# Norm factors as one VectorE operation and an inverse square root on GpSimd, and P in operations of 512 columns, in a one-core decoder layer

## Chip, cores and metric

The kernel runs on one core of a Trainium2 chip. The metric is the device time of one execution in microseconds. The kernel before took 3062.6 us (median of three runs, 3057.56 to 3067.12).

## The reference

One decoder layer on x of 4 x 512 tokens and 512 features: a gated delta-rule attention, a WKV recurrence over a second input and a routed feed-forward layer, each followed by a residual sum and a layer norm. The change touches only the attention:

```
q, k = l2norm(q) * DK**-0.5, l2norm(k)          # l2norm(x) = x / sqrt(sum(x*x) + 1e-6)
for each token:                                 # 32 heads, state Sm of 128 x 128 each
    Sm = Sm * exp(g)
    delta = (v - k @ Sm) * beta
    Sm = Sm + outer(k, delta)
    o = q @ Sm
og = o * silu(z)
on = og * rsqrt(mean(og*og) + EPS) * norm_w     # over the 128 features of a head
out = on @ w_out
```

The kernel works with q and k as they come and puts their lengths in later. With n2 = sum(q*q) + 1e-6 and ss = sum(og*og) of the unscaled output, the factor on og is

    1 / sqrt(ss / 128 + EPS * 128 * n2)  =  sqrt(128) / sqrt(ss + EPS * 128**2 * n2)

## The kernel before

Setup splits x into a high and a low part for exact products in three matmuls and makes the gates' decays. Then attention runs in 64 rounds and one tail does WKV, feed-forward and the three norms.

An attention unit s is one of 16 key heads (with its two value heads) and one of four chunks of 128 tokens, for all four batches. Round r of the loop works on three units at once: the state, the output and the output projection of unit r ("state"), the block inverse of unit r+1 ("solve"), and the projections, the convolution and the gates of unit r+2 ("ahead"). Each engine has its own in-order list of steps for a round, written out by hand (for TensorE from line 597, ScalarE 829, VectorE 1111, GpSimd 1213); the engines meet in semaphores that count upwards. The loop's order on each queue is all the scheduling there is.

The steps around the change:

- *gram* (VectorE, line 909): n2 is the lengths of the four k and four q per token (columns 4 to 7 are q's), r2 its reciprocal, cf and cfl the factors of delta. Then M (line 933), eight operations, and P (line 941), four operations: the products q k of PSUM times the decays E. M goes to DRAM and comes back as N in blocks; *base* (line 944) waits for it. TensorE's *by_token* (line 422) waits for each half of P, as it writes into the banks that P reads.
- *output* and *update* (lines 1029, 1047): O, the gated output, and the next state. ScalarE's *lengths* (line 746) squares O into ss.
- *taps* (line 1080): the convolution, three operations of 128x512 for each of the four projections j. Those of j = 1 stand partly ahead of the factors: all three in rounds with r mod 4 of 0 or 3, otherwise one ("early", line 1128).
- *factors* (VectorE, line 1060): f from ss and r2 in four dependent operations on 128x8. GpSimd's *factors* (line 1179) raises f to 0.5 and writes ron. ScalarE's *normed* (line 756, operation in line 763) scales O by ron into R. TensorE's *turn* (line 547, operation in line 551) transposes R, ScalarE's and VectorE's *turn* take it out of PSUM with a factor normw, and *out* (line 554) multiplies by w_out.
- behind the factors on VectorE: the remaining taps of j = 1 and those of j = 2, then *turn_T* (line 985) and *x_part* (line 994) of the block inverse. Xc (line 998) is what TensorE's *y_part* (line 449, operation in line 457) waits for; X itself comes from *x_part* on TensorE (lines 439 and 446).
- ScalarE has the SiLU of j = 1 (*silu*, line 799, operation in line 810) right ahead of *normed*; it waits for the last tap of j = 1.
- Line 409 transposes k and q of the next unit; its second half waits for Ut (line 702), the end of the block inverse. GpSimd also splits weights (line 1204) and keeps the convolution's halo (1193, 1199).

Of the kernel before, what the change touches and what calls it, by code (L numbers as in the profile page):

```python
# [9 lines left out]
ALU = mybir.AluOpType  # L10
# [3 lines left out]
B, S, D = 4, 512, 512  # L14
HV, HK, DH = 32, 16, 128
HJ = HV // HK
C = 128
# [11 lines left out]
EPS_NORM, EPS_LN = 1e-6, 1e-5  # L29
# [20 lines left out]
def decoder_kernel(nc, a, out):  # L50
    with ExitStack() as ctx:
        t, names = {}, []

        def sb(scope, name, *shape, dtype=F32):
            full = f"{name}_{len(names)}"
            names.append(full)
            t[name] = scope.enter_context(nc.sbuf_tensor(full, list(shape), dtype))
            return t[name]
# [9 lines left out]
        sb(ctx, "acc", 128, B, NC, D)  # L68
        sb(ctx, "eye4", 128, 4, 128)
        sb(ctx, "half", 128, 8)  # L70
        sb(ctx, "mhalf", 128, 4)
        sb(ctx, "ln", 128, 3, B, 12)
        for name, rows_, size in (("wkv_w", 128, KT), ("wkv_u", 128, KT), ("w_rows", KT, 128)):
            sb(ctx, name, rows_, size)
# [57 lines left out]
def setup(nc, a, t, banks, scratch, on):  # L132
# [95 lines left out]
    def vector(dve):  # L228
        def low(c):
            dve.wait_ge(on["xs_hi"], c + 1)  # L230
            dve.tensor_tensor(split("lo", c), t["xT"][:, c], split("hi", c), ALU.subtract).then_inc(on["xs_lo"], 1)

        for c in range(NC):
            low(c)
        dve.wait_ge(on["exs"], 1)
        dve.tensor_scalar(negA[:], negA[:], -1.0, None, ALU.mult).then_inc(on["gates"], 1)
        dve.wait_ge(on["exs"], 4)
        dve.tensor_scalar(wr[:], ex[:], 1.0, None, ALU.add).then_inc(on["w_plus"], 1)
        dve.wait_ge(on["ln"], 1)
        dve.tensor_scalar(wr[:], wr[:], -1.0, None, ALU.add).then_inc(on["gates"], 1)  # L240
        dve.wait_ge(on["gates"], 2)
        dve.tensor_scalar(tiny[:], wr[:], 0.0, None, ALU.is_equal).then_inc(on["gates"], 1)
        dve.wait_ge(on["gates"], 3)
        dve.tensor_tensor(wr[:], wr[:], tiny[:], ALU.add).then_inc(on["gates"], 1)
        dve.wait_ge(on["gates"], 4)
        dve.tensor_tensor(lg[:], lg[:], tiny[:], ALU.add).then_inc(on["gates"], 1)
        dve.wait_ge(on["gates"], 5)
        dve.reciprocal(wr[:], wr[:]).then_inc(on["gates"], 1)
        dve.wait_ge(on["gates"], 6)
        dve.tensor_tensor(lg[:], lg[:], wr[:], ALU.mult).then_inc(on["gates"], 1)  # L250
        dve.wait_ge(on["gates"], 7)
        dve.tensor_tensor(lg[:], lg[:], ex[:], ALU.mult).then_inc(on["gates"], 1)
        dve.wait_ge(on["gates"], 8)
        dve.scalar_tensor_tensor(out=yrow[:], in0=yrow[:], scalar=0.0, in1=lg[:], op0=ALU.max, op1=ALU.add).then_inc(on["gates"], 1)
        dve.memset(wr[:], 0.0).then_inc(on["gates"], 1)
        dve.wait_ge(on["gates"], 10)
        dve.wait_ge(on["exs"], 5)
        dve.tensor_copy(chunks(wr)[:, :, 0:1], chunks(ex)[:, :, 0:1]).then_inc(on["gates"], 1)
        dve.wait_ge(on["gates"], 11)
        dve.memset(chunks(ex)[:, :, 0:1], 0.0).then_inc(on["gates"], 1)  # L260
        dve.wait_ge(on["gates"], 12)
        dve.tensor_tensor_scan(cum[:], ex[:], wr[:], 0.0, ALU.mult, ALU.add).then_inc(on["cums"], 1)
        dve.wait_ge(on["cums"], 1)
        dve.tensor_copy(t["ends"][:], chunks(cum)[:, :, C - 1])

    with nc.Block() as block:  # L266
        block.sync(sync)
# [6 lines left out]
def attention(nc, a, t, banks, scratch, on):  # L274
# [7 lines left out]
    by2 = lambda ap: ap.rearrange("p (b j) -> p b j", j=HJ)  # L282
# [20 lines left out]
    n2, r2, nk = (lambda s: of(s, 0)), (lambda s: of(s, 8)), (lambda s: of(s, 16, 4))  # L303
    cf, cfl = (lambda s: of(s, 24)), (lambda s: of(s, 32))
    ncum = lambda s, b, j: tok[:, b, s % NC, 0, s // NC, j:j + 1]
    two = lambda name, s: t[f"{name}{s % 2}"]
# [350 lines left out]
    def scalar(act):  # L657
# [88 lines left out]
        def lengths(s):  # L746
            act.wait_ge(on["SD"], 2 * grown(s + 1))
            if s:
                act.wait_ge(on["f"], 4 * (s - 1) + 1)
            for half in range(2):  # L750
                act.wait_ge(on["og"], 2 * s + half + 1)
                for u in range(4 * half, 4 * half + 4):
                    op = act.activation(De[:, u // HJ, u % HJ], O[:, u // HJ, u % HJ], ACT.Square, accum_out=t["ss"][:, u:u + 1])
                op.then_inc(on["ss"], 1)
# [74 lines left out]
        for r in range(-3, NS):  # L829
# [27 lines left out]
            if state:  # L857
                lengths(r)
# [30 lines left out]
    def vector(dve):  # L889
# [19 lines left out]
        def gram(s):  # L909
# [13 lines left out]
            for half in range(2):  # L923
                b4 = solve_bank(half)[:].rearrange("p (b k s) -> p b k s", b=2, k=2)
# [5 lines left out]
                for i in range(2):  # L930
                    b = 2 * half + i
                    for j in range(HJ):
                        op = dve.scalar_tensor_tensor(out=t["M"][:, b, j], in0=b4[:, i, 0], scalar=cf(s)[:, 2 * b + j:2 * b + j + 1],
                                                      in1=t["E"][:, j, b], op0=ALU.mult, op1=ALU.mult)
                op.then_inc(on["M"], 1)
            for half in range(2):
                b4 = solve_bank(half)[:].rearrange("p (b k s) -> p b k s", b=2, k=2)
                if half == 0 and s >= 2:
                    dve.wait_ge(on["PD"], 2 * (s - 2) + 2)
                for j in range(HJ):  # L940
                    op = dve.tensor_tensor(two("P", s)[:, 2 * half:2 * half + 2, j], b4[:, :, 1], t["E"][:, j, 2 * half:2 * half + 2], ALU.mult)
                op.then_inc(on["P"], 1)

        def base(s):

# [112 lines left out]
                op.then_inc(on["S_next"], 1)  # L1058

        def factors(s):  # L1060
            f, r2q = t["f"], r2(s)[:, 4:8].unsqueeze(2).broadcast_to([128, B, HJ])
            dve.wait_ge(on["ss"], 2 * s + 2)
            dve.wait_ge(on["r2"], s + 1)
            if s:
                dve.wait_ge(on["ron"], s)
            dve.tensor_tensor(by2(f[:]), by2(t["ss"][:]), r2q, ALU.mult).then_inc(on["f"], 1)
            dve.wait_ge(on["f"], 4 * s + 1)
            dve.tensor_scalar(f[:], f[:], 1.0 / DH, EPS_NORM * DH, ALU.mult, ALU.add).then_inc(on["f"], 1)
            dve.wait_ge(on["f"], 4 * s + 2)
            dve.reciprocal(f[:], f[:]).then_inc(on["f"], 1)  # L1070
            dve.wait_ge(on["f"], 4 * s + 3)
            dve.tensor_tensor(by2(f[:]), by2(f[:]), r2q, ALU.mult).then_inc(on["f"], 1)

        def out(s, b):
            if s + b == 0:
# [35 lines left out]
        for r in range(-2, NS):  # L1111
# [3 lines left out]
            if solve:  # L1115
                gram(r + 1)
# [49 lines left out]
    def gpsimd(pool):  # L1166
# [10 lines left out]
            pool.tensor_tensor(t["wout_lo"][:, j], wout_raw[:, j], t["wout_hi"][:, j], ALU.subtract).then_inc(on["wout_lo"], 1)  # L1177

        def factors(s):
            pool.wait_ge(on["f"], 4 * s + 4)  # L1180
            if s:
                pool.wait_ge(on["on"], 2 * s)
            pool.tensor_tensor(t["ron"][:], t["f"][:], t["half"][:], ALU.pow).then_inc(on["ron"], 1)  # L1183

        def before(s, j):
            xb, halo, n = t["xb"][:, j], t["halo"][:, j], 4 * s + j
# [19 lines left out]
        def norm1(c):  # L1206
            st = t["ln"][:, c]
            pool.wait_ge(on["ln_stats"], 10 * c + 10)
            pool.tensor_tensor(st[:, :, 9], st[:, :, 8], t["mhalf"][:], ALU.pow).then_inc(on["ln_rstd"], 1)
            pool.wait_ge(on["ln_rstd"], 2 * c + 1)  # L1210
            pool.tensor_tensor(st[:, :, 11], st[:, :, 9], st[:, :, 10], ALU.mult).then_inc(on["ln_rstd"], 1)

# [584 lines left out]
```

## Time and profile before

| | |
|---|---|
| median of three runs | 3062.6 us |
| the profiled execution | 3062.48 us |
| its span | 3060.7 us |
| setup | 0 to about 54 us |
| attention loop | about 54 to 2699 us |
| tail | about 2699 us to the end |

The span is what the profiler sees between the first and the last instruction. An engine's idle time stands in front of the instruction that follows it, with the instruction that ended it. Operations of one engine can overlap by some tens of nanoseconds, so that merged rows ("x4") take less than the count times the mean.

### The profile page before, as it was taken

Reading aid. Unit: us, or ns where it says so; the run is one execution under the profiler, and the core shown is the slowest. Engines: PE = TensorE matmul, PEld = TensorE weight load, DVE = VectorE, ACT = ScalarE, POOL = GpSimd, SP = SyncE. Lnnn points to the kernel's source line nnn. Section 1 sums busy time; section 2 is a strip of 40 time slices with the busy share of each in tenths; the row PEclk is TensorE's granted clock in tenths of the full one; section 3 lists DMA queues with packets and bytes.
Section 4 is the critical chain, followed back from the end, with each engine's and each line's share of the span. In section 5 each row is a group of like instructions: output and inputs, shape, how many; then the busy total and the mean of one; then the engine's idle time right before and its main releaser. Section 6 shows DMA issues by size and latency. Waiting matters only on the chain. (4 is left out here: it accounts for less than half of the span.)

```text
span 3060.7 us, 78831 instructions
## 1 busy us (share of the span) xinstructions
PE 2884.2 (94%) x28584; PEld 2369.2 (77%) x28584; DVE 2663.7 (87%) x6377; ACT 1941.1 (63%) x6331; POOL 613.6 (20%) x902
## 2 busy tenths in 40 slices
PE   6899999999999999999999999999999999749998
PEld 4788887888888888888888888888888888636665
DVE  4698988999898889888989898988889898879995
ACT  3576666676767676666766666666676766544442
POOL 1121212121212112121212111212121221132221
PEclk9899999999999999999999999999999999869999
DMA  6434433343334343434334333334344433120000
GB/s 255 136 97 110 122 105 117 103 122 108 106 100 124 106 123 101 122 95 118 90 108 123 109 116 108 115 109 121 86 120 110 123 102 101 32 93 25 28 19 18
DMA packets 498474, 315.75 MB, mean 103 GB/s; under 512 B 314150, under 2 KB 453542, under 8 KB 480424
## 3 DMA queue, kind: packets, MB, share of 16 engines
q1 hardware_dynamic: 498088, 310.70, 34.6%
q8 instruction: 231, 3.78, 0.5%
q14 instruction: 155, 1.27, 0.1%
HBM read 243.07 MB, written 50.73 MB: 96 GB/s over the span
## 5 line engine op out<-in xcount | busy, mean ns | idle before, releaser
L1088 DVE SCALAR_TENSOR_TENSOR conv<-xb,convw,conv 128x512 f32<-128x512 f32 x768 | 592.0, 774 | 81.0 <-ACT conv L797 66.2
L580 PE MATMUL bank<-x_hi,w_hi 128*128 128x512 f32 x1024 | 429.7, 420 | 9.7 <-PEq L266 6.3
L580 PE MATMUL bank<-x_hi,w_lo 128*128 128x512 f32 x1024 | 403.2, 394 | 0.0
L580 PE MATMUL bank<-x_lo,w_hi 128*128 128x512 f32 x1024 | 400.5, 391 | 0.0
L791 ACT ACTIVATE xb<-bank 128x512 f32<-128x512 f32 x256 | 161.3, 630 | 302.7 <-PE bank L580 278.1
L592 PE MATMUL bank<-w_hi,x_hi 128*128 128x256 f32 x1024 | 304.4, 297 | 3.8 <-ACT conv L797 3.7
L592 PE MATMUL bank<-w_hi,x_lo 128*128 128x256 f32 x1024 | 290.4, 284 | 1.0 <-issue 1.0
L592 PE MATMUL bank<-w_lo,x_hi 128*128 128x256 f32 x1024 | 290.5, 284 | 0.0
L1171 POOL TENSOR_TENSOR small<-small,half 128x4 f32<-128x4 f32 x64 | 64.5, 1007 | 1034.2 <-DVE small L915 1034.2
L1199 POOL COPY halo<-xb 128x12 f32<-128x12 f32 x256 | 90.2, 352 | 839.3 <-ACT xb L791 839.0
L580 PEld LDWEIGHTS bank<-x_hi,w_hi 128*128 128x128 f32 x1024 | 194.1, 190 | 47.1 <-issue 9.0
L565 PE MATMUL bank<-wout_hi,onT_hi 128*128 128x512 f32 x512 | 230.0, 449 | 0.4 <-issue 0.4
L580 PEld LDWEIGHTS bank<-x_hi,w_lo 128*128 128x128 f32 x1024 | 193.3, 189 | 43.6
L580 PEld LDWEIGHTS bank<-x_lo,w_hi 128*128 128x128 f32 x1024 | 194.5, 190 | 37.5
L592 PEld LDWEIGHTS bank<-w_hi,x_hi 128*128 128x128 f32 x1024 | 195.8, 191 | 13.9 <-ACT conv L797 6.2
L565 PE MATMUL bank<-wout_hi,onT_lo 128*128 128x512 f32 x512 | 202.9, 396 | 0.0
L565 PE MATMUL bank<-wout_lo,onT_hi 128*128 128x512 f32 x512 | 202.7, 396 | 0.0
L592 PEld LDWEIGHTS bank<-w_lo,x_hi 128*128 128x128 f32 x1024 | 196.5, 192 | 2.5
L592 PEld LDWEIGHTS bank<-w_hi,x_lo 128*128 128x128 f32 x1024 | 196.5, 192 | 1.2 <-issue 1.2
L810 ACT ACTIVATE conv<-conv 128x512 f32<-128x512 f32 x128 | 80.1, 626 | 171.0 <-DVE conv L1088 169.0
L797 ACT ACTIVATE conv<-bank,convw 128x512 f32<-128x512 f32 x256 | 183.7, 718 | 3.2 <-DMA convw<-in_conv_w 3.2
L763 ACT ACTIVATE R<-O,ron 128x128 f32<-128x128 f32 x512 | 156.7, 388 | 32.9 <-POOL ron L1183 30.3
(276 smaller groups left out, 7643.6 us busy)
## 6 DMA issues: line engine op xcount, KB each, us to landing
x_hi<-x_hi_scratch SPq DMA_DIRECT2D x63, 1024.0 KB, 5.0
x_lo<-x_lo_scratch SPq DMA_DIRECT2D x63, 1024.0 KB, 8.2
E<-decay_scratch SPq DMA_DIRECT2D x64, 512.0 KB, 5.2
M_scratch<-M SPq DMA_DIRECT2D x128, 256.0 KB, 2.4
w_raw<-in_w_proj SPq DMA_DIRECT2D x64, 384.0 KB, 8.5
U<-Ut SPq DMA_DIRECT2D x256, 64.0 KB, 2.0
w_raw<-in_w_out SPq DMA_DIRECT2D x32, 256.0 KB, 3.0
Mt<-M_scratch SPq DMA_DIRECT2D x256, 32.0 KB, 1.9
```

The lines of the kernel that those rows point to most:

```text
L565: mm = pe.matmul(banks[4 + b][:], lhsT=t[f"onT_{p}"][:, j, b, :], rhs=t[f"wout_{q}"][:, j, :], start=i + j == 0, stop=i + j == len(PAIRS))
L580: mm = pe.matmul(banks[j % 2][:].rearrange("p (b t) -> p b t", b=B), lhsT=t[f"w_{p}"][:, k, j, :], rhs=t[f"x_{q}"][:, k], start=i == 0, st ...
L592: mm = pe.matmul(banks[half][:, i * 256:(i + 1) * 256], lhsT=t[f"x_{p}"][:, k, b, :], rhs=t[f"w_{q}"][:, k, 4:6, :], start=n == 0, stop=n ...
L763: op = act.activation(R[:, b, j], O[:, b, j], ACT.Copy, scale=t["ron"][:, HJ * b + j:HJ * b + j + 1])
L791: act.activation(xb[:, :, TAPS - 1:], bank[:].rearrange("p (b t) -> p b t", b=B), ACT.Copy).then_inc(on["xb"], 1)
L797: act.activation(y, bank[:], ACT.Copy, scale=t["convw"][:, j, TAPS - 1:]).then_inc(on["y"], 1)
L810: act.activation(dst, y3, ACT.Silu).then_inc(on["silu"], 1)
L1088: dve.scalar_tensor_tensor(out=y3, in0=xb[:, :, i:i + C], scalar=t["convw"][:, j, i:i + 1], in1=y3, op0=ALU.mult, op1=ALU.add).then_inc(on ...
L1171: pool.tensor_tensor(nk(s), n2(s)[:, 0:4], t["half"][:, 0:4], ALU.pow).then_inc(on["nk"], 1)
L1199: pool.tensor_copy(halo, xb[:, :, C:C + TAPS - 1]).then_inc(on["save"], 1)
```

## The change

The four operations of *factors* on VectorE become one scalar_tensor_tensor, f = n2 * (EPS * 128 * 128) + ss. GpSimd raises it to -0.5 in place of 0.5, on the same shape. The missing factor sqrt(128) goes into normw, which setup scales once. The operand mhalf grows to eight columns. The semaphore f now counts one per round in place of four, and its waits follow. The step waits for n2 in place of r2; both are written in *gram* long before. And P is made in two operations of 128x512 in place of four of 128x256; the first operand is read from PSUM with the two value heads j as a broadcast dimension.

```diff
@@ setup, vector
+        dve.wait_ge(on["d_in"], 32)
+        dve.tensor_scalar(t["normw"][:], t["normw"][:], float(np.sqrt(DH)), None, ALU.mult)
@@ attention, scalar, lengths
-                act.wait_ge(on["f"], 4 * (s - 1) + 1)
+                act.wait_ge(on["f"], s)
@@ attention, vector, gram
-                for j in range(HJ):
-                    op = dve.tensor_tensor(two("P", s)[:, 2 * half:2 * half + 2, j], b4[:, :, 1], t["E"][:, j, 2 * half:2 * half + 2], ALU.mult)
-                op.then_inc(on["P"], 1)
+                dve.tensor_tensor(two("P", s)[:, 2 * half:2 * half + 2], b4[:, :, 1].unsqueeze(2).broadcast_to([128, 2, HJ, C]),
+                                  t["E"][:, :, 2 * half:2 * half + 2].rearrange("p j b s -> p b j s"), ALU.mult).then_inc(on["P"], 1)
@@ attention, vector, factors
-            f, r2q = t["f"], r2(s)[:, 4:8].unsqueeze(2).broadcast_to([128, B, HJ])
             dve.wait_ge(on["ss"], 2 * s + 2)
-            dve.wait_ge(on["r2"], s + 1)
+            dve.wait_ge(on["n2"], s + 1)
             if s:
                 dve.wait_ge(on["ron"], s)
-            dve.tensor_tensor(by2(f[:]), by2(t["ss"][:]), r2q, ALU.mult).then_inc(on["f"], 1)
-            dve.wait_ge(on["f"], 4 * s + 1)
-            dve.tensor_scalar(f[:], f[:], 1.0 / DH, EPS_NORM * DH, ALU.mult, ALU.add).then_inc(on["f"], 1)
-            dve.wait_ge(on["f"], 4 * s + 2)
-            dve.reciprocal(f[:], f[:]).then_inc(on["f"], 1)
-            dve.wait_ge(on["f"], 4 * s + 3)
-            dve.tensor_tensor(by2(f[:]), by2(f[:]), r2q, ALU.mult).then_inc(on["f"], 1)
+            dve.scalar_tensor_tensor(out=by2(t["f"][:]), in0=n2(s)[:, 4:8].unsqueeze(2).broadcast_to([128, B, HJ]), scalar=EPS_NORM * DH * DH,
+                                     in1=by2(t["ss"][:]), op0=ALU.mult, op1=ALU.add).then_inc(on["f"], 1)
@@ attention, gpsimd, factors
-            pool.wait_ge(on["f"], 4 * s + 4)
+            pool.wait_ge(on["f"], s + 1)
-            pool.tensor_tensor(t["ron"][:], t["f"][:], t["half"][:], ALU.pow).then_inc(on["ron"], 1)
+            pool.tensor_tensor(t["ron"][:], t["f"][:], t["mhalf"][:], ALU.pow).then_inc(on["ron"], 1)
```

## Rows read from the trace of the kernel before

**Rows 1.** The page: each engine's busy us, share of the span and instructions.
```profile
PE 2884.2 (94%) x28584; PEld 2369.2 (77%) x28584; DVE 2663.7 (87%) x6377; ACT 1941.1 (63%) x6331; POOL 613.6 (20%) x902
```

**Rows 2.** Busy us of PE, PEld, DVE, ACT, POOL; granted clock; DMA share, GB/s.
```profile
130.00:2640.00 2510.00, 2438.77 (x26414) 2067.77 (x26414) 2251.62 (x5617) 1716.90 (x5848) 494.38 (x739) 1.00 0.38 109
```

**Rows 3.** TensorE's waits from 130 to 2640 us: total us, times, longest.
```profile
PE bank L457 <- DVE Xc L998: 20.7, 30, 1.2
PE bank L551 <- ACT R L763: 19.5, 26, 1.4
PE bank L409 <- ACT Ut L702: 10.0, 15, 0.7
PE bank L427 <- DVE P L941: 5.0, 16, 1.0
```

**Rows 4.** Timeline of one round: start us, us, instruction, idle before it and releaser.
```profile
1197.13 0.16 DVE L1066 TENSOR_TENSOR f<-ss,small 128x8 f32<-128x8 f32 x1
...
1197.85 3.77 DVE L1088 SCALAR_TENSOR_TENSOR conv<-xb,convw,conv 128x512 f32<-128x512 f32 x5
1198.02 2.08 POOL L1183 TENSOR_TENSOR ron<-f,half 128x8 f32<-128x8 f32 x1 [1.49 <-DVE f L1072]
...
1199.42 0.63 ACT L810 ACTIVATE kq<-conv 128x512 f32<-128x512 f32 x1 [1.03 <-DVE conv L1088]
1200.13 2.45 ACT L763 ACTIVATE R<-O,ron 128x128 f32<-128x128 f32 x8
...
1201.55 0.63 PE L551 MATMUL bank<-eye,R 128*128 128x128 f32 x4 [0.78 <-ACT R L763]
1201.90 0.39 DVE L998 TENSOR_TENSOR Xc<-bank,level 128x256 f32<-128x256 f32 x1
...
1202.34 0.76 PE L457 MATMUL bank<-Xc,Uc 32*32 32x32 f32 x64 [0.16 <-DVE Xc L998]
```

**Rows 5.** Timeline: first and last of 46 idle rounds; one round with ScalarE idle.
```profile
186.42 0.75 PE L457 MATMUL bank<-Xc,Uc 32*32 32x32 f32 x64 [1.21 <-DVE Xc L998]
...
265.76 2.45 ACT L763 ACTIVATE R<-O,ron 128x128 f32<-128x128 f32 x8 [1.62 <-POOL ron L1183]
...
267.18 0.63 PE L551 MATMUL bank<-eye,R 128*128 128x128 f32 x4 [0.87 <-ACT R L763]
...
2577.47 0.26 PE L457 MATMUL bank<-Xc,Uc 32*32 32x32 f32 x6 [1.18 <-issue]
```

**Rows 6.** Powers on GpSimd, by line (min/median/max ns) and group (mean ns).
```profile
L1183 POOL TENSOR_TENSOR ron<-f,half x64: 1635/2076/2081, 140.3 to 2685.2; 128x8 f32<-128x8 f32 x64
L1209 POOL TENSOR_TENSOR ln<-ln,mhalf x3: 1008/1010/1010, 2640.3 to 2684.0; 128x4 f32<-128x4 f32 x3
L1171 POOL TENSOR_TENSOR small<-small,half 128x4 f32<-128x4 f32 x64 | 64.5, 1007 | 1034.2 <-DVE small L915 1034.2
L1725 POOL TENSOR_TENSOR a<-base_e,a 128x4 f32<-128x4 f32 x1 | 1.4, 1379 | 0.7 <-DVE a L1524 0.7
```

**Rows 7.** VectorE's groups by shape, the whole span or the loop: busy us, mean ns.
```profile
L1078 DVE TENSOR_TENSOR acc<-bank,acc 128x512 f32<-128x512 f32 x256 | 169.0, 682 | 7.3 <-PE bank L565 5.4
L941 DVE TENSOR_TENSOR P<-bank,E 128x256 f32<-128x256 f32 x256 | 90.2, 416 | 0.0
L979 DVE TENSOR_TENSOR prods<-T,W 64x512 f32<-64x512 f32 x64 | 77.5, 1211 | 2.2
L954 DVE SCALAR_TENSOR_TENSOR prods<-N,T 64x8 f32<-64x8 f32 x61 | 9.6, 158 | 0.0
```

**Rows 8.** Timeline: P, and two operations of the 512-column form in a row.
```profile
1253.92 1.26 DVE L1078 TENSOR_TENSOR acc<-bank,acc 128x512 f32<-128x512 f32 x2
...
1258.93 1.41 DVE L941 TENSOR_TENSOR P<-bank,E 128x256 f32<-128x256 f32 x4
```

**Rows 9.** VectorE's waits over the whole span: total us, times, longest.
```profile
DVE T L951 <- DMA N<-M_scratch: 57.5, 58, 3.2
```

**Rows 10.** Busy time and granted clock of one stretch, columns as in rows 2.
```profile
349.40:352.80 3.40, 3.40 (x45) 2.81 (x44) 2.10 (x5) 1.52 (x3) 0.00 (x0) 0.50 0.43 96
```

More of the change, by code:

```diff
@@ L70, in decoder_kernel @@
         sb(ctx, "half", 128, 8)
-        sb(ctx, "mhalf", 128, 4)
+        sb(ctx, "mhalf", 128, 8)
         sb(ctx, "ln", 128, 3, B, 12)
@@ L1208, in norm1 @@
             pool.wait_ge(on["ln_stats"], 10 * c + 10)
-            pool.tensor_tensor(st[:, :, 9], st[:, :, 8], t["mhalf"][:], ALU.pow).then_inc(on["ln_rstd"], 1)
+            pool.tensor_tensor(st[:, :, 9], st[:, :, 8], t["mhalf"][:, 0:B], ALU.pow).then_inc(on["ln_rstd"], 1)
             pool.wait_ge(on["ln_rstd"], 2 * c + 1)
```

## The prediction

> **What bounds the kernel now.** I read the totals of the page first, then the busy time by stage, then TensorE's waits, then single rounds of the timeline. TensorE is busy 94% of the span and VectorE 87% [rows 1]. The middle of the attention loop, from 130 to 2640 us, is 2510 us long, and TensorE is busy for 2438.8 us of it at a granted clock that rounds to full speed [rows 2]. So in 62 rounds of about 40 us only 71 us are not TensorE's own work. Work that this change removes from VectorE is not worth its own length: it is worth what it takes out of these 71 us, and nothing else. The reader should therefore ask of each edit which of TensorE's waits it shortens.
>
> The table of waits names them [rows 3]. The longest two are the product of the block inverse (line 457) waiting for VectorE's Xc, 20.7 us in 30 waits, and the transposes of the normed output (line 551) waiting for ScalarE's R, 19.5 us in 26 waits. Then come 10.0 us for Ut (line 409) and 5.0 us for P (line 427).
>
> One round shows that the first two hang on one place in VectorE's order of work [rows 4]. VectorE starts the norm factors at 1197.13 and begins the next tap at 1197.85, so the four dependent operations take 0.72 us. GpSimd starts its power at 1198.02 and ScalarE the scaling of R at 1200.13, right behind it; TensorE, idle for 0.78 us, starts its transposes at 1201.55. VectorE itself runs through five taps, the transpose and Xc without a gap, and Xc (1201.90) releases line 457 at 1202.34 after a further 0.16 us of idle. In another kind of round there is no idle ahead of Xc either, but ScalarE has nothing else to wait for: it stood 1.62 us until the factors of GpSimd were there [rows 5].
>
> **The change, part by part.** *Norm factors.* Before, the operations start at 1197.13 and the next VectorE operation at 1197.85. Afterwards there is one small operation. The nearest row is the scalar_tensor_tensor of line 954, 158 ns [rows 7]; a broadcast operand does not show in it, but line 1066 has one and its row in the round is 0.16 us too [rows 4]. As line 1066 does with an operation that does not depend on it, the next tap can begin a little before the end, at about 0.09 us. So VectorE's queue moves 0.72 - 0.09 = 0.63 us earlier from there on, and so does the start of the power: both ends of the chain, R and Xc, move by the same 0.63 us. The price from both sides: if the next tap has to wait for the full end and a semaphore, the shift is 0.55; it can't be above 0.72.
>
> *The power.* It has the same shape, 128x8, but the exponent is -0.5 and the operand another. Its time is 2076 ns in nearly all rounds and 1635 ns at the least [rows 6]. The pattern of the round explains both: taps follow each other at 3.77/5 = 0.754 us, the power starts 0.17 after the first, so 1.64 us of its own would end at 1199.66, and it ends at 1200.10, where the third tap ends (1197.85 + 3 x 0.754 = 1200.11) [rows 4]. It ends with a tap because it waits for one. As tap and power move together by 0.63, this phase stays, and so does 2.08. The exponent: a power by -0.5 of 128x4 took 1008 to 1010 ns three times, in line with 1007 for the power by 0.5 of that shape; a power of the same 128x4 with other operands took 1379 [rows 6]. I take no change, and keep 37% as the upper bound for a rival.
>
> Here the Trainium skill has a rule (page "SBUF — State Buffer", section "SBUF: two separate sides"): a GpSimd operation and a VectorE operation with two SBUF inputs hold a shared port pair exclusively, and the loser is blocked for the whole instruction. The trace agrees that GpSimd loses up to 0.44 us, but not that a power blocks taps: the five taps beside it keep 0.754 us each. Under the strict rule the power would push one tap back by its full 1.64 us, before and after alike.
>
> *What the 0.63 us are worth.* The waits have to be taken one by one, since a wait of 0.16 us can give back only 0.16. I listed every idle of TensorE in front of lines 551 and 457 from 130 to 2640 us: 46 rounds have one, the first at 186.42, the last at 2577.47 (one of two whose releaser the view leaves open; I count both) [rows 5]. In each round the gain is the smaller of 0.63 and the idle at both lines together. Of the 26 rounds with an idle at line 551, 18 reach 0.63, which is 11.3 us, and eight give 0.22 to 0.61, together 3.5 us. Of the 20 with one at line 457 alone, 11 (about 1.2 us each) give 0.63, 6.9 us, and nine give 0.16, 1.5 us. Sum: 23.2 us. In the other rounds VectorE only gets ahead and waits later: it already stands 57.5 us in 58 rounds for the block N from DRAM [rows 9], a wait that hangs on M and not on anything that is made shorter here.
>
> What is late next? ScalarE's SiLU of the second projection ends at 1200.05, only 0.05 before the power does [rows 4]. It was itself released by a tap that stands behind the factors, so it moves too. GpSimd could be the next limit only if it were not idle before the power; it waits for f before it. For line 409 I count nothing: its chain starts behind line 457 and moves rigidly with it.
>
> *P.* Four operations of 256 columns, 416 ns each, become two of 512 with one operand in PSUM; line 1078 has that form and takes 682 ns, the same form at 128x512 [rows 7]. Durations would say 1664 - 1364 = 0.30 us per round. But operations that don't depend on each other overlap: four of P take 1.41 us on the engine and two of line 1078 take 1.26 [rows 8]. So it is 0.15 us. It moves the block solve nowhere, since VectorE waits for N right after [rows 9]. It shortens line 427's waits, 16 of them, 5.0 us in all [rows 3]: 16 x 0.15 = 2.4 us, between 0 and 5.0.
>
> The Trainium skill's VectorE page ("VectorE: DVE Perf Modes", section "The TRN2 errata — SBUF-src ops pay a fixed extra latency per instruction") gives 120 cycles of fixed cost for an operation that reads PSUM, at 0.96 GHz. An estimate from that page: two operations fewer save 0.25 us a round, 16 us in 64 rounds if VectorE were the bound. The rows of this case show 0.15 us of engine time, and most of that in front of a wait.
>
> *The rest.* The extra scaling of normw in setup is one column wide, behind the last scan; I count 0. The operand mhalf of eight columns costs nothing.
>
> *The clock.* TensorE's granted clock falls to half (1.2 of 2.4 GHz) for 3.4 us just behind rounds with long idle: from 349.40 to 352.80 it is 0.50 [rows 10], and there are five such stretches between 130 and 2640 us. Each follows within 3 us a round where TensorE stood 1.5 to 2.2 us in front of these two lines (the first of them 0.91 and then 1.21 us); two other rounds with 2.0 and 2.4 us have none. A stretch costs at most 3.4/2 = 1.7 us, five 8.5 us. The change takes 0.63 off the idle ahead of each. From 0 to 8.5, I take half, 4.2 us.
>
> **Sum.** 23.2 + 2.4 + 4.2 = 29.8 us. The profiled execution took 3062.48 us (its span 3060.7), the median of the runs is 3062.6, so no correction between them: 3062.5 - 29.8 = 3032.7, say **3033 us**.
>
> **Rivals.**
> 1. *The gain comes, but the clock gives nothing or P nothing:* 3062.5 - 23.2 = 3039; with all five stretches gone and all of line 427's waits, 3062.5 - 36.7 = 3026. These are inside my forecast.
> 2. *ScalarE's order takes the wait over.* If its SiLU did not move, of line 551's rounds only those where ScalarE stood idle for the factors would gain, 15 of the 26 and 7.4 us; line 457 does not hang on ScalarE and keeps its 8.4: 3062.5 - 7.4 - 8.4 - 2.4 = 3044 us. For it: the two end 0.05 apart [rows 4]. Against it: the SiLU waits for a tap behind the factors. Chance 0.10.
> 3. *VectorE's gain is not in TensorE's waits:* they are filled by something that I don't see (a DMA, or the next wait in the round, such as line 409's), and only P's 2.4 us are left: 3060 us. For it: 71 us of idle in 2510 is little, and many chains run side by side. Against it: behind line 457 all that TensorE waits for starts from line 457 itself. Chance 0.12.
> 4. *Slower: the power on GpSimd.* If the new operands made it longer, the end of a tap sets how much. Up to 0.44 us more is free, since it ends at the same tap; by the 37% of the row of 1379 ns it would grow by 0.6 and end one tap later, so that R comes 0.75 - 0.63 = 0.12 us later than now: 26 x 0.12 = 3 us lost against 8.4 + 2.4 gained, 3054 us. From 1.2 us more on it ends two taps later, R comes 0.87 us late, and at least the 26 rounds lose that: 3062.5 + 22.6 - 2.4 = 3083 us, the gain at line 457 being hidden behind 551. Against it: the 1009 ns at -0.5. Chance 0.04, of which 0.03 slower.
> 5. *P costs more than its columns.* 512-element operations with awkward access take 1211 ns here (line 979) against 682 [rows 7]. P would then take about 2.3 instead of 1.41 us, and in the 16 rounds with no cover 0.9 us each are lost: 14 us, 3062.5 - 23.2 + 14 = 3053 us. Its inner runs are 128 contiguous columns in both forms, which speaks against it. Chance 0.04.
>
> **How the numbers follow.** Forecast 0.70, rival 2 0.10, rival 3 0.12, rival 4 0.04, rival 5 0.04. The predicted time is the forecast's. The range has to hold 8 in 10: from 3023 (all terms at their upper bound, 3026, less some scatter of the runs, which spread over 9.6 us) to 3055 (rivals 2 and 5 inside, which leaves out rivals 3 and 4 and some of the forecast's own error). Below 0.3%, 9.2 us, this measurement can't tell from no change: 3053.4 to 3071.8 is the same. Faster holds the forecast but for 0.03 given away, rival 2 and half of rival 5: 0.79. The same holds rival 3, half of 5, the small case of 4 and the 0.03: 0.18. Slower is the large case of 4: 0.03.
>
> **What the profile after would show.** One row of about 0.16 us in the place of lines 1066 to 1072, and the next tap about 0.1 us after its start. The power at 2.08 us as before and its exponent without effect. The waits of line 551 fall from 19.5 to about 6 us and those of line 457 from 23 (with the two open ones) to about 14, since in rounds with both the one at 457 stays while its moment moves; line 427's from 5.0 to about 3. P in two rows of about 0.68 us. TensorE's busy time from 130 us to the end of the loop unchanged but for fewer stretches of 0.5 clock, while the stretch itself gets shorter; VectorE's wait for N longer by some 0.15 us a round. I am wrong if the waits at 551 and 457 stay although the factors are 0.63 us earlier, if the power's duration moves, or if the waits go and others (409, 439) grow by as much.

## The result, and the profile after

The changed kernel takes 3034.8 us (median of four executions, 3031.6 to 3037.9), the kernel before 3061.3 us beside it: ratio 0.9923, 95% interval 0.9906 to 0.9940. (The ratios are those on record; they are not the quotients of the two medians, which would be 0.9913 here.) Measured again in another session it was 3031.7 us beside 3063.1, and 0.9900 (0.9881 to 0.9919). The prediction was 3033 us, in a range from 3023 to 3055. The profiled execution took 3034.04 us, with a span of 3032.3 us against 3060.7. All ratios leave out one single execution, the sixth of experiment 6, which took 15768 us for a reason that nothing here shows.

The page's busy times and the stretch of the loop that answers to [rows 1, 2]:

```profile
PE 2877.5 (95%) x28584; PEld 2367.5 (78%) x28584; DVE 2624.8 (87%) x6058; ACT 1937.2 (64%) x6331; POOL 617.3 (20%) x902
130.00:2612.00 2482.00, 2433.13 (x26424) 2067.13 (x26423) 2214.55 (x5310) 1714.38 (x5853) 498.14 (x739) 1.00 0.38 110
```

VectorE lost 39 us of work, and the span 28 us. TensorE did the same 28584 matmuls. In the loop it stood idle for 49 us where it had stood for 71.

TensorE's waits from 130 to 2620 us, for [rows 3] (line 459 was 457, 553 was 551, 411 was 409, 429 was 427):

```profile
PE bank L459 <- DVE Xc L999: 13.4, 19, 1.2
PE bank L411 <- ACT Ut L704: 10.4, 15, 0.7
PE bank L553 <- ACT R L765: 4.5, 14, 0.7
PE bank L459 <- issue: 3.6, 3, 1.7
PE bank L429 <- DVE P L942: 3.6, 16, 0.6
```

The two waits that were forecast to fall fell: for R from 19.5 to 4.5 us, for Xc from 20.7 to 13.4. The wait for Ut, which was said to move rigidly with line 457, did not change (10.0 and 10.4 us).

The timeline of one round, for [rows 4]:

```profile
1187.02 0.19 DVE L1066 SCALAR_TENSOR_TENSOR f<-small,ss 128x8 f32<-128x8 f32 x1
1187.13 3.78 DVE L1083 SCALAR_TENSOR_TENSOR conv<-xb,convw,conv 128x512 f32<-128x512 f32 x5
1187.29 2.09 POOL L1178 TENSOR_TENSOR ron<-f,mhalf 128x8 f32<-128x8 f32 x1
...
1189.54 2.44 ACT L765 ACTIVATE R<-O,ron 128x128 f32<-128x128 f32 x8
...
1191.36 0.60 PE L553 MATMUL bank<-eye,R 128*128 128x128 f32 x4
...
1191.89 0.75 PE L459 MATMUL bank<-Xc,Uc 32*32 32x32 f32 x64
```

From the start of f to the first tap there are 0.11 us (0.72 before), and the power takes 2.09 us (2.08 before). Both of the idles in front of lines 551 and 457 are gone. R starts 2.52 us after f, where it was 3.00: it gained 0.48 us and not 0.61.

The power is not the same in every round. In 17 of the 64 (12 in the second profile of this kernel) it starts 0.8 us or more after f and takes 1.63 us. In 15 of them (all of the kind called 0 below) GpSimd's own copy of the halo comes in between, which before had been done by the time f was ready. The copy in one such round before, and the same place after:

```profile
300.29 0.19 POOL L1199 COPY halo<-xb 128x12 f32<-128x12 f32 x1 [1.55 <-ACT xb L791]
```

```profile
300.71 0.16 DVE L1066 SCALAR_TENSOR_TENSOR f<-small,ss 128x8 f32<-128x8 f32 x1
300.79 2.32 DVE L1083 SCALAR_TENSOR_TENSOR conv<-xb,convw,conv 128x512 f32<-128x512 f32 x3
300.85 0.74 POOL L1194 COPY halo<-xb 128x12 f32<-128x12 f32 x1 [1.58 <-ACT xb L793]
301.55 1.64 POOL L1178 TENSOR_TENSOR ron<-f,mhalf 128x8 f32<-128x8 f32 x1
```

The copy, 0.19 us long before, now starts 0.06 us into a tap and ends 0.05 us behind it, after 0.74 us, and the power starts behind it. Its end comes 2.47 us after f's start in place of 2.36, so this costs some 0.1 us of R's shift in these rounds.

And P, for [rows 8]:

```profile
1247.67 1.28 DVE L942 TENSOR_TENSOR P<-bank,E 128x512 f32<-128x512 f32 x2
...
1248.40 1.26 PE L429 MATMUL bank<-eye,conv 128*128 128x128 f32 x8 [0.20 <-DVE P L942]
```

The sharpest view is the length of a round, taken between two starts of line 439 (441 after) on TensorE. The same round of both kernels, first before, then after:

```profile
1482.24 0.25 PE L439 MATMUL bank<-Tc,M 32*32 32x32 f32 x6
1524.82 0.26 PE L439 MATMUL bank<-Tc,M 32*32 32x32 f32 x8
```

```profile
1466.78 0.45 PE L441 MATMUL bank<-Tc,M 32*32 32x32 f32 x32
1508.73 0.45 PE L441 MATMUL bank<-Tc,M 32*32 32x32 f32 x32
```

42.58 became 41.95: 0.63 us, the shift that was forecast for VectorE's queue. Rounds repeat in four kinds, numbered here from the first such start. The table has the median round of each kind, and the sum from the first start to the last but one, each from one profiled execution (kernels of the experiments stand here too, with the number of the experiment):

| kernel | kind 0 | kind 1 | kind 2 | kind 3 | 62 rounds |
|---|---|---|---|---|---|
| before | 38.51 | 40.19 | 42.58 | 39.61 | 2511.5 |
| after | 38.05 | 40.19 | 41.95 | 38.93 | 2482.2 |
| after, second time (3) | 38.18 | 40.19 | 41.96 | 39.06 | 2481.8 |
| factors alone (1) | 38.05 | 40.19 | 41.93 | 38.79 | 2472.3 |
| factors alone, second time (4) | 38.03 | 40.20 | 41.95 | 38.77 | 2482.6 |
| delay behind f (5) | 37.95 | 40.19 | 42.45 | 39.18 | 2493.5 |
| delay ahead of f (6) | 38.39 | 40.19 | 42.48 | 39.11 | 2502.5 |
| Xc one tap earlier (9) | 37.96 | 40.18 | 41.16 | 38.98 | 2465.3 |
| P twice (12) | 38.97 | 40.19 | 41.94 | 38.75 | 2484.4 |

Kind 1 has no wait at either line in 14 of its 16 rounds and gains nothing (40.19 both times): VectorE got ahead there and waited, its listed idle in the 16 rounds growing from 55.5 to 63.2 us. The other three kinds gain 8.4, 10.8 and 12.0 us; kind 1 loses 1.9, nearly all in two odd rounds. The sum is 29.3 us. (The first such start comes 1.9 us later than before, and what follows the last but one takes 1.1 us less; that makes the 28 us of the span.) The medians repeat to within 0.15 us from one execution of a kernel to the next, the sums do not: 2472.3 and 2482.6 us are the same kernel.

### The profile page after: what moved, and what is told of

It is laid out like the page before. It is cut to its first block and busy times, and to the rows that moved or that the text cites. A ratio compares the mean times of both kernels' runs of the same rounds, so it can differ in the third digit from the quotient of the medians.

```text
span 3032.3 us, 78512 instructions
## 1 busy us (share of the span) xinstructions
PE 2877.5 (95%) x28584; PEld 2367.5 (78%) x28584; DVE 2624.8 (87%) x6058; ACT 1937.2 (64%) x6331; POOL 617.3 (20%) x902
## 5 line engine op out<-in xcount | busy, mean ns | idle before, releaser
L1083 DVE SCALAR_TENSOR_TENSOR conv<-xb,convw,conv 128x512 f32<-128x512 f32 x768 | 591.9, 774 | 89.7 <-ACT conv L799 74.9
L1194 POOL COPY halo<-xb 128x12 f32<-128x12 f32 x256 | 103.7, 405 | 840.3 <-ACT xb L793 840.3
L1073 DVE TENSOR_TENSOR acc<-bank,acc 128x512 f32<-128x512 f32 x256 | 169.0, 681 | 7.5 <-PE bank L567 5.5
```

Source lines behind the costliest of these rows:

```text
L1073: dve.tensor_tensor(t["acc"][:, b, s % NC, :], banks[4 + b][:], t["acc"][:, b, s % NC, :], ALU.add).then_inc(on["acc"], 1)
L1083: dve.scalar_tensor_tensor(out=y3, in0=xb[:, :, i:i + C], scalar=t["convw"][:, j, i:i + 1], in1=y3, op0=ALU.mult, op1=ALU.add).then_inc(on ...
L1194: pool.tensor_copy(halo, xb[:, :, C:C + TAPS - 1]).then_inc(on["save"], 1)
```

## The experiments

**1. The factors alone** (P as before):

```diff
-                dve.tensor_tensor(two("P", s)[:, 2 * half:2 * half + 2], ...  # 512 columns
+                for j in range(HJ):
+                    op = dve.tensor_tensor(two("P", s)[:, 2 * half:2 * half + 2, j], b4[:, :, 1], t["E"][:, j, 2 * half:2 * half + 2], ALU.mult)
+                op.then_inc(on["P"], 1)
```

> The changed kernel with P as before, in four operations of 256 columns. Theory (the place of the factors in VectorE's order is what pays): about 25 us of the 26.5 stay, ratio to the kernel before 0.992 to 0.993 (3036 us), TensorE's waits for R and Xc as in the changed kernel (about 4.5 and 13 us), the wait for P back at 0.27 us each. Rival (the gain is VectorE's total load, of which P's operations are a part: P's rows fell from 90 to 82 us, the factors from 45 to 11): about four fifths of the gain, 3040 us, and the waits for R and Xc in between.

3029.9 us, ratio 0.9905 (0.9888 to 0.9922): the whole gain, without P's new form. TensorE's waits, 130 to 2610 us:

```profile
PE bank L459 <- DVE Xc L1000: 12.6, 18, 1.2
...
PE bank L429 <- DVE P L943: 4.7, 16, 0.6
...
PE bank L553 <- ACT R L765: 3.6, 12, 0.6
```

**2. P alone** (before.py with the two operations of 512 columns):

> The kernel before with only P in two operations of 512 columns. Theory: 1 to 2.4 us (3059 to 3060 us), the waits for P 0.20 instead of 0.27 us each, the waits for R and Xc as before (19.5 and 20.7 us) since VectorE waits for the block N behind P. Rival (VectorE's load counts): 5 us, the waits for R and Xc shorter.

3061.8 us, ratio 1.000 (0.9989 to 1.001). The waits for R and Xc are nearly those of before, and the wait for P fell all the same, from 5.0 us in 16 waits (130 to 2640 us):

```profile
PE bank L457 <- DVE Xc L997: 20.6, 30, 1.2
PE bank L551 <- ACT R L763: 17.1, 24, 1.4
...
PE bank L427 <- DVE P L940: 3.9, 16, 0.8
```

So P's part is worth nothing that can be measured; up to 3 us either way stay possible. Where its 0.14 us a round go is seen in VectorE's waits. Right behind P stand the taps of j = 0, and in 46 rounds (kinds 1 to 3) they wait for ScalarE's conv; the wait for N stands behind them. First before, then P alone, both from 130 to 2640 us:

```profile
DVE conv L1088 <- ACT conv L797: 44.5, 46, 1.0
```

```profile
DVE T L950 <- DMA N<-M_scratch: 54.2, 62, 3.5
DVE conv L1087 <- ACT conv L797: 51.1, 46, 1.1
```

The wait for conv is 45.2 and 45.1 us in the two executions with the factors alone and 50.9 and 50.8 in the two of the changed kernel, so it hangs on P's form. The wait for N (54.7 us before in this stretch) did not grow with P.

The first two measurements seemed to say that the 512 columns even cost something, 3029.9 us without them against 3034.8 with them, but they come from different sessions. So both were measured again, side by side on one chip.

**3. The changed kernel again, 4. the factors alone again:**

> The changed kernel unchanged, beside the one with the factors alone on the same chip. Theory: both within 3 us of each other, near 3035 and 3032 us; the number of stretches at half clock in the loop differs from kernel to kernel and takes or gives 1.7 us each. Rival (P in 512 columns costs something): the changed kernel is slower by 4 us or more with an interval clear of the other.

> The kernel with the factors alone again. Theory: 3030 to 3035 us, within 3 us of the changed kernel. Rival: 4 us or more faster than it, as the first measurement suggested (0.9905 against 0.9923).

3031.7 us (0.9900, 0.9881 to 0.9919) and 3036.2 us (0.9918, 0.9897 to 0.9939). Now the order is the other way round. The difference of 4 to 5 us between the two was scatter and not P.

**5. A delay behind the factors.** The changed kernel with three dependent operations of 0.2 us on a small tile of their own (three tensor_scalar on dum, 128x8, each waiting for the one before). The delay is work added.

```diff
             if state:
                 factors(r)
+                idle_ops(r)
```

> The changed kernel with three dependent small operations on a tile of their own (about 0.6 us) on VectorE right behind the factors. VectorE's load is that of before in time, R can come early only where ScalarE's SiLU does not wait for a tap behind them, Xc comes as late as before. Theory: only rounds with a wait for R and none for Xc gain, 7.2 us, and P's 1 to 2: 3052 us; the 1.2 us waits for Xc are back. Rival (the load counts, or everything hangs on Xc): 3059 us, as in the kernel with the delay ahead of the factors.

**6. The same delay ahead of the factors.**

> The same three operations ahead of the factors. Theory: R and Xc are as late as before, nearly all of the gain is gone: 3058 to 3060 us, the waits for R 19 us and for Xc 20 us. Rival (the gain came from fewer semaphore steps between VectorE and GpSimd or from the other operand of the power): it stays below 3050 us.

3045.5 us (0.9945, 0.9927 to 0.9964) with the delay behind f, 3051.1 us (median of five; 0.9960, 0.9946 to 0.9974) with the delay ahead of it. The executions of the two overlap (3037.1 to 3050.0 and 3044.6 to 3054.3), so that their times alone do not tell them apart for certain; both lie well above the factors alone in the same session (3029.9). Waits of the first, then of the second kernel, both 130 to 2610 us:

```profile
PE bank L459 <- DVE Xc L999: 22.2, 30, 1.4
...
PE bank L553 <- ACT R L765: 7.9, 10, 1.0
```

```profile
PE bank L459 <- DVE Xc L999: 20.6, 30, 1.2
PE bank L553 <- ACT R L765: 17.5, 26, 1.2
```

The waits are what the place says. With the delay ahead of the factors both are nearly back at their values of before, although f itself is still one operation and the power has its new operand. With the delay behind, Xc is as late as before and R is early. So neither the fewer semaphore steps nor VectorE's load made the gain, but the two moments at which f and Xc are there. The kinds of rounds show it for each of the two. Kind 0 waits for R and not for Xc: it is as short as in the changed kernel with the delay behind f (37.95 against 38.05), and nearly as long as before with the delay ahead of it (38.39 against 38.51). Kind 2 waits above all for Xc: it is as long as before both times, but for 0.1 us (42.45 and 42.48 against 42.58). Both times are lower than I expected, by 6 us or more. The trace of the first has a round in which the power is shorter:

```profile
1193.36 0.16 DVE L1066 SCALAR_TENSOR_TENSOR f<-small,ss 128x8 f32<-128x8 f32 x1
1193.43 0.60 DVE L1072 TENSOR_SCALAR dum<-dum 128x8 f32<-128x8 f32 x3
1193.94 3.77 DVE L1088 SCALAR_TENSOR_TENSOR conv<-xb,convw,conv 128x512 f32<-128x512 f32 x5
...
1193.59 1.64 POOL L1185 TENSOR_TENSOR ron<-f,mhalf 128x8 f32<-128x8 f32 x1 [0.84 <-DVE f L1066]
...
1195.50 0.63 ACT L812 ACTIVATE kq<-conv 128x512 f32<-128x512 f32 x1 [0.92 <-DVE conv L1088]
1196.04 2.44 ACT L765 ACTIVATE R<-O,ron 128x128 f32<-128x128 f32 x8
```

The power took 1.64 us, not 2.08. (What follows from this for the power stands below.) But in this round R did not come earlier by it: the power ended at 1195.23, and R starts at 1196.04, behind ScalarE's SiLU, which waits for a tap behind the delay. That is 2.68 us after f, later than the 2.52 of the changed kernel. Only in kind 3 does R follow the shorter power (1.92 us after f, 2.35 in the changed kernel; medians). So the shorter power explains a part of it at most.

For the second, part is the delay being 0.11 us shorter than the three operations that it stands for (at the median 0.61 us from the start of the delay to the first tap, 0.72 before), in some 45 rounds, 5 us. Its profiled execution also has three stretches at half clock in the loop where the kernel before has five, up to 3.4 us. Together these come to 8 us, which is the lower end of the interval of its gain over the kernel before; the median gain is 10.

**7. One operation behind f.** The same with one operation in place of three, in one execution.

> The changed kernel with one small operation of 0.2 us on VectorE behind the factors, ahead of the taps. In the kernel with three of them the power took 1.64 us instead of 2.08. Two readings: (a) the power is held at its start by the tap in flight (0.44 us), and here it starts about 0.25 us after f's start, before the tap (0.29): it takes 1.64 us. (b) It is held at its end until a tap ends, as the prediction had it: started at 0.25, it would end with the second or third tap of a row that starts at 0.29, at 1.8 or 2.55, so 2.3 us or, by a narrow miss, 1.6 in a few rounds only. By (a) R comes 0.44 us earlier and Xc 0.2 later than in the changed kernel: waits for R near 1 us in all, for Xc up by 3 to 4.

3039.4 us. The edit did not do what I wanted: the operation does not depend on f and costs only 0.08 us, so the tap was there before the power after all.

```profile
1189.96 0.16 DVE L1072 TENSOR_SCALAR dum<-dum 128x8 f32<-128x8 f32 x1
1190.04 3.76 DVE L1088 SCALAR_TENSOR_TENSOR conv<-xb,convw,conv 128x512 f32<-128x512 f32 x5
1190.12 2.15 POOL L1185 TENSOR_TENSOR ron<-f,mhalf 128x8 f32<-128x8 f32 x1
```

Still it gives a point. Started 0.16 us after the tap, the power takes 2.09 us (changed kernel); started 0.08 after it, 2.15; started 0.35 ahead of it (experiment 5), 1.64. The first two fit a hold at the start as well as one at the end. The third fits only the start: it ended at 1195.23, in the middle of the tap that ran from 1194.69 to 1195.45. The copy of the halo, held for just the rest of a tap, says the same.

**8. The factors one tap earlier.** They stand ahead of the first tap of j = 1, or ahead of the third where all three came first.

```diff
-            early = TAPS - 1 if r % NC in (0, NC - 1) else 1
+            first = 2 if r % NC in (0, NC - 1) else 0
```

> The changed kernel with the factors one tap (0.75 us) earlier in VectorE's order in every round: ahead of the first tap of j = 1, or ahead of the third in rounds that had all three before. Xc stays where it is. Theory (two chains, each with its own waits; the later one counts): the waits for R vanish (4.5 us, with what the modelled ends cover about 6), but in rounds with both waits Xc takes them over: 2 to 4 us faster than the changed kernel, 3031 to 3033 us, ratio 0.990 to 0.992. Rival (R is the chain that counts, since the change moved it): over 10 us faster.

3033.6 us, ratio 0.9911 (0.9882 to 0.9939): next to nothing, as I expected, but not for the reason that I gave. TensorE's waits, 130 to 2600 us:

```profile
PE bank L459 <- DVE Xc L999: 16.6, 20, 1.4
...
PE bank L553 <- ACT R L765: 3.7, 11, 0.7
```

The wait for R hardly fell (4.5 to 3.7 us), and that for Xc grew by 3 us (13.4 to 16.6). The edit moved f, but it did not move R:

```profile
227.25 0.17 DVE L1066 SCALAR_TENSOR_TENSOR f<-small,ss 128x8 f32<-128x8 f32 x1
...
227.76 0.37 POOL L1194 COPY halo<-xb 128x12 f32<-128x12 f32 x1 [2.57 <-ACT xb L793]
228.09 1.63 POOL L1178 TENSOR_TENSOR ron<-f,mhalf 128x8 f32<-128x8 f32 x1
...
230.32 2.44 ACT L765 ACTIVATE R<-O,ron 128x128 f32<-128x128 f32 x8
```

GpSimd's copy of the halo stands ahead of the power in its order and waits for ScalarE's xb; in 53 of the 64 rounds the power starts over 0.8 us after f. R starts 3.07 us after f here, against 2.52 in the changed kernel (3.06 against 2.35 in kind 3), so that of the tap by which f moved, 0.75 us, at most 0.2 is left for R in kinds 1 to 3 (the SiLU on ScalarE comes between the power and R here). This experiment does not show what an earlier R would be worth.

**9. Xc one tap earlier.** The last tap of j = 2 moves behind the first half of *x_part*, and ScalarE takes the first half of *turn* ahead of the SiLU of j = 2, which now comes later.

```diff
-                taps(r + 2, 2)
+                taps(r + 2, 2, (0, 1))
             if solve:
                 turn_T(r + 1, 0)
                 x_part(r + 1, 0)
             if ahead:
+                taps(r + 2, 2, (2,))
                 taps(r + 2, 3, (0,))
@@ scalar
-            if ahead:
-                silu(r + 2, 2)
             if state:
-                turn(r)
+                turn(r, (0,))
+            if ahead:
+                silu(r + 2, 2)
+            if state:
+                turn(r, (1,))
```

> The changed kernel with the last tap of j = 2 moved behind the first part of the block inverse, so that Xc comes 0.75 us earlier, and ScalarE's first half of turn ahead of its SiLU of j = 2, which is now later. Theory: the waits for Xc (17 us with the ones whose releaser is open) fall to about 5; 8 to 12 us faster than the changed kernel, 3023 to 3027 us. Rival (the later tap delays ScalarE and with it the output projection, lines 565 and 409 or their like): the waits move there and the time stays at 3035 us or goes up.

3018.9 us, ratio 0.9870 (0.9830 to 0.9909), 13 to 16 us below the changed kernel, more than I expected. Its four executions (3016.2 to 3026.1) all lie below the ten of the changed kernel (3027.5 to 3037.9). Waits, 130 to 2600 us:

```profile
PE bank L553 <- ACT R L765: 5.4, 16, 0.8
...
PE bank L459 <- DVE Xc L1001: 1.7, 4, 0.4
```

The waits for Xc are nearly gone, 13.4 to 1.7 us, and those for R grew by 1 us only. The median round of kind 2 fell from 41.95 to 41.16 us. VectorE does the same operations in another order, so this gain is one of Xc's moment and of no load. After the change Xc's chain is the one that ends last, then. The two edits, VectorE's and ScalarE's, were not tried one without the other.

**10. Both, and the ends of the loop.** Experiments 8 and 9 together; besides, the norm statistics of chunk 1 moved to the last round, and in that round the factors stand ahead of the statistics of chunk 2, on VectorE and on GpSimd.

```diff
-            if r == NS - 2:
+            if r == NS - 1:
                 norm1(1)
@@
-            if r == NS - 1:
-                norm1(2)
             if state:
                 factors(r)
+            if r == NS - 1:
+                norm1(2)
```

> Both orders together, and in the last two rounds the norm statistics of chunks 1 and 2 moved out of the way of the gated output and the factors (VectorE and GpSimd). Theory: the two chains add up where they stood together (5 rounds with both waits give 0.75 to 1.2 us more), the ends give 3 us each: 3008 to 3016 us. Rival (ends hidden behind the chain from DRAM): 3018 to 3022 us.

3012.8 us, ratio 0.9849 (0.9811 to 0.9887). It beats both kernels: 48 us below the one before, some 20 below the changed one. The two orders did not add up as I had expected: the 62 rounds take 2465.6 us in its profile, as in experiment 9 (2465.3), and what follows them 439.3 us in place of 444.2. The 6 us that it gains over experiment 9 come from the end of the loop, as far as one profile each can tell.

**11. The same with P in four operations** (the diff of experiment 1 on top):

> The kernel with both orders and the ends moved, with P in four operations of 256 columns. Theory: 3010 to 3016 us, as with P in 512 columns (3013); the waits for P 0.27 instead of 0.20 us. Rival (P matters once the other waits are gone): slower by 3 us or more.

3014.6 us, ratio 0.9844 (0.9821 to 0.9868). P's form makes no difference here either.

**12. P done twice.** Each of P's two operations is issued twice in a row, the second behind a wait for the first.

> The changed kernel with each of P's two operations done twice, the second behind the first: about 1.5 us more on VectorE ahead of its wait for N. Theory: 16 rounds have no cover at line 429 and lose 1.5 us each, 24 us; in the others VectorE comes 1.5 us late to a wait of about 0.9 us for N, so that R and Xc are some 0.6 us late and most of the change's gain goes too, about 20 us: near 3079 us. Rival (the wait for N takes it all): only the 24 us, 3059 us.

```diff
+                dve.tensor_tensor(two("P", s)[:, 2 * half:2 * half + 2], ...).then_inc(on["dum"], 1)
+                dve.wait_ge(on["dum"], 2 * s + half + 1)
                 dve.tensor_tensor(two("P", s)[:, 2 * half:2 * half + 2], ...).then_inc(on["P"], 1)
```

3041.7 us, ratio 0.9940 (0.9918 to 0.9962): 7 us over the first measurement of the changed kernel and 10 over the second, which was in the same session; I had forecast 24 or 44. The waits, TensorE's from 130 to 2600 us and VectorE's for N over the whole span:

```profile
PE bank L429 <- DVE P L945: 24.6, 31, 0.9
PE bank L459 <- DVE Xc L1002: 11.2, 16, 1.2
```

```profile
DVE T L955 <- DMA N<-M_scratch: 15.6, 23, 1.7
```

The stall for P is there, 21 us of it, and kind 0 is 0.92 us longer at the median (38.97 against 38.05). But the kinds without such a wait are as long as in the changed kernel (40.19 and 41.94): there VectorE's lateness vanished in its own waits, and that part of the theory was wrong. VectorE has 86 us more work; its wait for N fell from 51.8 to 15.6 us and its wait for ScalarE's conv from 74.9 to 22.9, 88 us together. TensorE's other waits (lines 459, 553, 441 and 594 above all) fell by some 10 us (that for R from 4.5 to 2.1), and the stretches at half clock in the loop went from four to none, which is up to 7 us. In the profiled executions the 62 rounds take only 2.2 us more than in the changed kernel (2484.4 against 2482.2) where the span is 7.4 longer; the other 5 lie before the first and behind the last of these rounds. Whether the stall itself brought the clock's share was not tested.

## Why the prediction was right, point by point

- *TensorE sets the time, and only its waits pay:* right. Kind 1, without a wait at these lines, gained 0.0 us at the median although VectorE's queue is 0.6 us shorter in it.
- *The shift of 0.63 us:* right for Xc. 0.08 to 0.12 us remain of 0.72, and kind 2 is 0.63 us shorter. R moved with it only in kind 3 (2.35 us after f in place of 3.00, medians); in kinds 1 and 2 it gained 0.50 and in kind 0 0.3 to 0.4 us, because ScalarE and GpSimd had other work in front of it. The delays of experiments 5 and 6 show that the moments of R and of Xc count, each by itself, and experiment 9 shows it for Xc again.
- *23.2 us at lines 551 and 457:* the listed idle fell from 42.8 (with the two open ones) to 21.5 us, 21.3. The time lost in a wait is more than its listed idle, since the modelled end of the matmul ahead of it covers some of it: in the pair of rounds above the listed idle fell by 0.50 us and the round by 0.63. The rounds shrank by 29.3 us in sum. The listed idle of TensorE in them fell by 22 us in all and the clock gave 1.7; the rest would be such covered time, which is argued from single pairs of rounds and not shown for the sum.
- *P, 2.4 us:* mis-sized. The pair takes 1.28 against 1.41 us, but the first half, on which the wait hangs, is ready only 0.07 us sooner: 0.27 became 0.20. The waits fell by 1.4 us instead of 2.4 (15 of them by 0.07, one odd one by 0.4), and nothing of it shows in the time (0 +- 3 us alone). The forecast had VectorE wait for N right behind P, and this wait grow by 0.15 us a round. That reading of the order was wrong: the taps of j = 0 come first, and P's gain ends in their wait for ScalarE's conv (44.5 to 51.1 us with P alone). Over the whole span the wait for N was 57.5 us before and 51.8 and 56.4 in the two profiles of the changed kernel, so it did not grow.
- *The clock, 4.2 us:* mis-sized. The stretches at half clock between the same marks went from five to four in the profiled executions, 1.7 us. One of them:

```profile
471.30:474.70 3.40, 3.40 (x39) 2.33 (x38) 2.06 (x7) 2.40 (x6) 0.00 (x0) 0.50 0.78 260
```

  The factors alone had none the first time and three the second; experiment 9, with the least waiting, had none. So a kernel's executions differ by some microseconds in this alone. The four that are left in the changed kernel stand behind rounds in which TensorE was idle for 1.5 to 2.0 us in front of the two lines, and before the five stood behind 1.5 to 2.2 us: 0.63 us less did not take the long idles away.
- *The power:* its duration was right in 46 of 64 rounds (51 in the second profile) and 1.63 us in the others, its reason wrong. I had it wait for the end of a tap before it ends; experiment 5 shows that it is held at its start by the tap in flight. Where it starts in the same place behind the start of the first tap, the 2.08 us came out the same. That GpSimd waits for nothing but f before it was wrong in kind 0, where the copy of the halo now comes late (0.74 us in place of 0.19). The Trainium skill's rule (page "SBUF — State Buffer", section "SBUF: two separate sides") that the loser waits for the holder's instruction agrees with 1.64 us ahead of the tap and 2.09 behind its start. Its other half, that the power then blocks the taps, is not seen: five taps take 3.77 us in experiment 5, though the power was already running when the first of them started.
- *The rivals:* ScalarE's order took a little over: in the round shown R starts at 1189.54, the power having ended at 1189.38, since the SiLU ahead of it was not done; that is 0.16 of the 0.63 us, and line 551 had no wait left there to notice. The same holds for the median of kinds 1 and 2. The exponent costs nothing: the shortest powers take 1.63 us, 1.64 before. Operations of P take 679 ns on average, not 1211.

The central figure is closer than its terms deserve, and that is luck: the stalls gave more than their listed idle, P and the clock gave less. The measurement is no sharper than that either: by the medians the gain was 26.5 us the first time and 31.4 the second, around the 29.8 that were forecast.

## What to carry to other kernels

List the bounding engine's waits one by one and give an edit, per wait, the smaller of its shift and the wait; a shift of 0.6 us on another engine was worth 0.0 in one kind of round and 0.63 in the next. When one operation releases two chains, look which of them ends last afterwards: here the next step that paid was to move one tap behind Xc (another 13 us or more). When an edit is meant to make a result earlier, read in the trace whether the result itself moved: the factors one tap earlier moved f and left R where it was, because GpSimd and ScalarE had other work in front of it. And do not add up stalls as if they were serial: twice P brought 21 us of new waits at line 429 and 7 to 10 us of time.

## What the runs showed of the hardware that was not expected

- A GpSimd power of 128x8 takes 1.64 us if it starts while no large VectorE operation with two SBUF operands runs, and 2.08 to 2.15 if it starts 0.17 to 0.08 us into a tap (128x512, both operands in SBUF): the rest of the tap, less about 0.14 us, is added. With the delay of experiment 5 its median is 1637 ns:

```profile
L1185 POOL TENSOR_TENSOR ron<-f,mhalf x64: 1634/1637/2128, 143.3 to 2668.7; 128x8 f32<-128x8 f32 x64
```

- A GpSimd copy of 128x12 that takes 0.19 us by itself took 0.74 when it started 0.06 us into a tap: it ended 0.05 us behind the tap.
- Not every GpSimd operation leaves the taps alone as the power does. Beside the subtract of line 1172 (128x512) in the changed kernel, a tap follows the one before after 1.18 us (median of 11), and after 0.79 where GpSimd does nothing.
- The listed idle of TensorE is less than the time lost where a wait only shrinks or goes. In the pair of rounds above it fell by 0.50 us and the round by 0.63; in kind 2 of experiment 9 the 0.72 us in front of line 459 are gone and the median round is 0.79 us shorter.
- A small VectorE operation that depends on nothing costs 0.08 us in the queue, a dependent one 0.2 (experiments 7 and 5).
